# Attention's first loads, buffers and the experts' table: another order and other engines

## Chip, cores and metric

One core of a Trainium2 chip runs the whole kernel. Five engines work side by side, each on its own list of instructions: TensorE (PE), VectorE (DVE), ScalarE (ACT), GpSimd (POOL) and SyncE (SP, which here only issues DMAs). They wait for each other through semaphores. The metric is the device time of one execution in microseconds (us).

## What is computed

A batch of 8 samples. Each has 49 image patches, projected and normalised, and 512 words, embedded and passed through four encoder layers; together 561 tokens of 192 values. On these comes an attention layer and a layer of eight experts:

```
h = concatenate([tok(x), txt(x_txt)], axis=1)          # 8 x 561 x 192
h = h + attn(layernorm(h))                             # 12 heads of 64, own token masked out
h = h + ffn(layernorm(h))                              # 8 experts, the best 2 of each token

# attn(x)
qkv = x @ W_qkv.T ; q, k, v = split(qkv, 3)            # 12 heads each
dots = einsum('bhid,bhjd->bhij', q, k) * scale[head]
dots = where(diagonal, -987654321.0, dots)
out = einsum('bhij,bhjd->bhid', softmax(dots), v)
return out @ W_out.T + b_out
```

## The kernel before

The program has three phases, each a block of its own in which every engine has its instruction list; a phase begins on all engines when the one before has ended on all of them: `encoder_phase` (0 to about 2281 us), `attention_phase` (to about 3690 us) and `experts_phase`. They hand data over in DRAM: `tokens` (encoder to attention), `fused` (attention to experts) and `table` (one row of weights per expert and partition, 1024 rows of 11.5 KB, read by the experts by index).

**The encoder's end.** Encoder work runs in turns of two samples (`s` 0 and 1) over a written order of steps; `R_FINAL` is the last turn and `R_CLOSE` what is left behind it. In `encoder_phase` the list of SyncE is the function `steps` of the `sync` block: at step ("exp", 1, 0, 1) it stores a finished sample (L839), then loads two rows of norm parameters (L810, `load_rows(..., norm2_in)`). In `R_FINAL` the next things on SyncE's list are the two last stores of `h_out` (calls of `store` behind `steps(R_FINAL, 0)`, L839 again). GpSimd waits for `stored` of the other `s` before it writes `h_out` anew (L756). At its end SyncE waits for the last stores (L947 and on).

**Attention.** One sample at a time (`B` = 8), each over 5 tiles of tokens (four of 128 rows, one of 49) and 12 heads. The regions are `R_AHEAD` (what must run before the first sample's loop body), `R_FIRST`, `R_SECOND`, a loop of five, `R_FINAL` and `R_CLOSE`. `R_AHEAD` holds, in order: ("ln", 0) moments and ("ln", 1) normalising of the tokens on VectorE (L1376 to L1385, with the reciprocal root on GpSimd, L49 and L51), ("t", 0/1) transposes on TensorE (L1231) that ScalarE copies to `xT` (L1333), ("qk", ...) products for the first four heads (L1240), from which ScalarE and VectorE write q and k as a high part and a rest (L1338, L1340, L1410, L1413), SyncE's copies between partitions (`place`, L1123 to L1127), then the maxima and sums of four heads (L1268, L1271, L1430, L1320), `lse` and `maxt`. The v products, which need `wv`, the output product, which needs `wo`, and the addition of `b_out` on GpSimd (L1189) come only in `R_FIRST` or behind it.

**The start of attention, engine by engine.**
- SyncE: loads `ident`, `wqk`, `wv`, `wo`, `b_out`, `scales` (L1165), each counted on `fixed_in`; then the tokens of sample 0 (`load(0, loaded)`, L1116 and L1117); waits for `ready` 3.
- VectorE: sets `q_hm` and `k_l1` to 0 (L1439), the last columns of `q_hl` and `k_hh` (L1441), `vals` and `probs` of the last tile (L1443), three small ones (L1445), then rows 64 and 65 of `k_l1` to 1 (L1447); waits for `fixed_in` 96 (all six loads) and makes `eye16` and `mask16` from `ident` (L1452, L1453). Each of the two large memsets, the ones in `k_l1`, `eye16` and `mask16` count one on `ready`.
- GpSimd: sets `half` (L1204), waits for `fixed_in` 96 and `ready` 5.
- TensorE: waits for the same two.
- ScalarE: first issues seven DMAs that build `table` from the inputs `wup_rows`, `wdown_rows`, `bdown` and `bup_rows`, DRAM to DRAM (L1362, counted on `made`), then waits for the same two.

SyncE waits for `made` at the end of attention. In `q_hm`, partitions 0 to 63 take a copy of q's high part, partitions 64 and 65 the shifts of the softmax, and the rest stay 0; in `k_l1`, partitions 0 to 63 take k's rest and 64 and 65 hold 1, against the shifts. A product of the two sums over all 128 partitions.

## Time and profile before

| | us |
|---|---|
| runs | 4368.18, 4368.94, 4373.55 |
| median | 4368.94 |
| the profiled execution, its own time | 4374.97 |
| its span, first to last instruction | 4373.2 |
| busy in the span: PE, DVE, ACT, POOL | 3810.5, 2232.9, 2119.3, 1101.8 |
| mean granted clock of TensorE, of full | 0.924 |

How to read the rows below. All times are us from the span's start unless ns is written. A row of the timeline is: start, length, engine, line of the kernel, operation, output <- input, shape, count; in brackets, how long the engine was idle before it and what ended that ("issue": nothing that the profile shows). "ACTq", "SPq" are the queues of DMA instructions of those engines: their length is the time for issuing, not for the transfer; neighbouring rows of one kind are merged, from the first's start to the last's end. L1441 and the like are lines of the listing. "PEclk" is the granted clock of TensorE as a share of 2.4 GHz. "DMA share" is the mean busy share of the core's sixteen DMA engines. A row of DMA issues ends with the us from issue to landing.

### The profile page before, as it was taken

The page shows a single profiled execution, that of the slowest core. Times are in us where ns is not written, and L with a number is a line of the kernel's source. Part 1 is how long each engine was busy: PE and PEld are TensorE (multiplying, and loading weights), DVE is VectorE, ACT ScalarE, POOL GpSimd, SP SyncE. Part 2 cuts the span into 40 slices and gives each one's busy share as a digit, 9 for nine tenths or more (in the row PEclk, how much of TensorE's full clock was granted, in tenths as well). Part 3 has the DMA queues.
Part 4 walks back from the last instruction along what each step waited for, and adds up shares of the span by engine and source line. Part 5 has one row for each costly group of instructions (what it writes and reads, how often), then busy time and mean ns, then how long its engine had stood idle before and what let it go on. Part 6 is the DMA issues. An engine that isn't in the chain of part 4 may idle for free. (4 is left out here: it accounts for less than half of the span.)

```text
span 4373.2 us, 64449 instructions
## 1 busy us (share of the span) xinstructions
PE 3810.5 (87%) x21850; PEld 2532.1 (58%) x21850; DVE 2232.9 (51%) x3419; ACT 2119.3 (48%) x3230; POOL 1101.8 (25%) x1004
## 2 busy tenths in 40 slices
PE   4899999999999999999856999999999996408998
PEld 2455555555555555555534677666766774307887
DVE  6566666666666666666524444444444442213443
ACT  0554554554555545545414766755756663003332
POOL 5132332322332322323210000000000001063444
PEclk7899999999999999999977999999999998558999
DMA  7333233242343342333114111111111112335664
GB/s 174 93 101 105 87 106 102 87 117 87 90 119 93 94 117 79 101 108 92 48 48 116 31 34 27 31 35 23 35 31 24 37 28 96 103 112 161 148 145 107
DMA packets 265492, 368.62 MB, mean 84 GB/s; under 512 B 49616, under 2 KB 166400, under 8 KB 261824
## 3 DMA queue, kind: packets, MB, share of 16 engines
q1 hardware_dynamic: 232752, 285.52, 23.1%
q0 software_dynamic: 22960, 57.40, 5.8%
q10 hardware_dynamic: 9600, 23.26, 1.6%
q8 instruction: 118, 1.93, 0.2%
q14 instruction: 62, 0.51, 0.0%
HBM read 235.77 MB, written 116.32 MB: 81 GB/s over the span
## 5 line engine op out<-in xcount | busy, mean ns | idle before, releaser
L641 DVE TENSOR_REDUCE mx<-ring 128x2 f32<-128x1024 f32 x768 | 920.0, 1223 | 505.8 <-PE ring L404 502.8
L533 ACT ACTIVATE probs<-ring 128x1024 f32<-128x1024 f32 x768 | 767.2, 1024 | 418.0 <-PE ring L417 417.0
L1430 DVE TENSOR_REDUCE a_nmx<-a_ring 128x1 f32<-128x561 f32 (+1 forms) x480 | 341.6, 737 | 309.1 <-PE a_ring L1271 158.9
L1320 ACT ACTIVATE a_ring<-a_ring,a_nmx 128x561 f32<-128x561 f32 (+1 forms) x480 | 333.8, 695 | 197.8 <-DVE a_nmx L1430 194.8
L404 PE MATMUL ring<-k_stack,q_stack 48*128 48x512 f32 x1536 | 360.0, 481 | 63.5 <-ACT probs L533 23.1
L417 PE MATMUL ring<-q_stack,k_stack 64*128 64x512 f32 x1536 | 363.5, 490 | 51.9 <-DVE mx L641 39.2
L431 PE MATMUL acc<-probs,vals 128*32 128x512 f32 x3072 | 400.6, 642 | 1.3 <-ACT probs L533 1.3
L1201 POOL TENSOR_SCALAR_AFFINE_SELECT a_probs<-a_probs 128x256 f32<-128x256 f32 (+1 forms) x240 | 91.9, 383 | 1227.4 <-ACT a_probs L1352 1227.4
L1352 ACT ACTIVATE a_probs<-a_ring 128x561 f32<-128x561 f32 (+1 forms) x480 | 287.4, 637 | 169.2 <-PE a_ring L1268 166.4
L1268 PE MATMUL a_ring<-a_k_hh,a_q_hl 128*128 128x256 f32 (+1 forms) x960 | 311.1, 339 | 22.6 <-DVE a_q_hl L1410 11.0
L417 PEld LDWEIGHTS ring<-q_stack,k_stack 64*128 64x128 f32 x1536 | 142.6, 189 | 285.9 <-DVE mx L641 102.0
L404 PEld LDWEIGHTS ring<-k_stack,q_stack 48*128 48x128 f32 x1536 | 145.5, 191 | 279.7 <-issue 84.7
L1268 PE MATMUL a_ring<-a_q_hl,a_k_hh 128*128 128x256 f32 (+1 forms) x960 | 288.7, 326 | 10.4 <-ACT a_ring L1320 7.6
L477 PE MATMUL ring<-w,relu 128*128 128x192 f32 x1536 | 279.7, 332 | 1.4 <-ACT relu L540 1.4
L1288 PE MATMUL a_acc<-a_probs,a_vals 128*64 128x305 f32 (+1 forms) x1920 | 275.1, 413 | 0.1
L1268 PE MATMUL a_ring<-a_k_l,a_q_hm 128*128 128x256 f32 (+1 forms) x960 | 272.1, 292 | 0.0
L477 PEld LDWEIGHTS ring<-w,relu 128*128 128x128 f32 x1536 | 246.3, 190 | 33.6 <-issue 31.1
L1268 PE MATMUL a_ring<-a_q_hm,a_k_l 128*128 128x256 f32 (+1 forms) x960 | 264.4, 292 | 0.0
L1240 PE MATMUL a_ring<-a_xT,a_wqk 96*128 96x256 f32 (+1 forms) x768 | 217.9, 432 | 23.0 <-issue 11.5
L49 POOL TENSOR_SCALAR var_eps<-mv 128x4 f32<-128x4 f32 (+1 forms) x65 | 14.9, 229 | 844.8 <-DVE mv L576 844.5
L1888 ACT ACTIVATE m_hid<-m_ring,m_table 128x512 f32<-128x512 f32 x150 | 103.0, 686 | 254.3 <-PE m_ring L1867 254.3
L1837 POOL DMA_INDIRECT fused<-m_y,m_ids x100 | 167.9, 1679 | 213.8 <-DVE m_y L1920 198.6
(220 smaller groups left out, 6801.8 us busy)
## 6 DMA issues: line engine op xcount, KB each, us to landing
q_stack<-qk_scratch SPq DMA_DIRECT2D x576, 64.0 KB, 2.3
k_stack<-qk_scratch SPq DMA_DIRECT2D x576, 64.0 KB, 2.4
qk_scratch<-qk_hi SPq DMA_DIRECT2D x32, 768.0 KB, 3.6
qk_scratch<-qk_lo SPq DMA_DIRECT2D x32, 768.0 KB, 5.1
a_q_hm<-a_q_hl SPq DMA_DIRECT2D x48, 280.5 KB
a_k_hh<-a_k_hh SPq DMA_DIRECT2D x48, 280.5 KB
tokens<-h_out SPq DMA_DIRECT2D x33, 384.0 KB, 2.5
h_in<-tokens SPq DMA_DIRECT2D x32, 384.0 KB, 4.3
```

Source lines behind the costliest of these rows:

```text
L404: last = nc.tensor.matmul(buf[:, r, :], q_st[s][terms, t, P * i:P * i + P], k_st[s][terms, t, :], start=True, stop=True)
L417: last = nc.tensor.matmul(buf[:, r, :], k_st[s][terms, t, P * kt:P * kt + P], q_st[s][terms, t, :], start=True, stop=True)
L431: last = nc.tensor.matmul(acc[g % 2][32 * hh:32 * hh + 32, :], vals[s][:, kt, 4 * (n // 2) + hh, :], probs[n % 2][:, hh, j, :], start=(n % ...
L477: last = nc.tensor.matmul(buf[:, i // 2, D * (i % 2):D * (i % 2) + D], relu[:, k2, P * i:P * i + P], w2[:, k2, :], start=(k2 == 0), stop=( ...
L533: nc.scalar.activation(probs[n % 2][:, pair:pair + 2, x // 2, :], buf[:, :, :], ACT.Exp, scale=DK ** -0.5).then_inc(act, 1)
L641: nc.vector.tensor_reduce(mx[s][:, i, :].rearrange("p (r t) -> p r t", r=2)[:, :, t], buf[:, :, :], AX, ALU.max).then_inc(dve, 1)
L1240: last = nc.tensor.matmul(flat(buf)[:, n0:n0 + n], wqk[:, c, P * j:P * j + P], xT[:, c, n0:n0 + n], start=(c == 0), stop=(c == 1))
L1268: last = nc.tensor.matmul(flat(buf)[0:r, n0:n0 + w], a, b[:, n0:n0 + w], start=(m == 0), stop=(m == 1 and not masked))
L1288: last = nc.tensor.matmul(flat(acc)[DH * r:DH * r + DH, n0:n0 + w], vals[:, i, 2 * p + r, :], probs[i][:, r, n0:n0 + w], start=(i == 0), s ...
L1320: nc.scalar.activation(buf, buf, ACT.Exp, bias=nmx[0:r, i, h:h + 1], accum_out=sums[0:r, i, h:h + 1]).then_inc(act, 1)
L1352: nc.scalar.activation(probs[i][0:r, h % 2, :], flat(buf)[0:r, 0:N], ACT.Exp).then_inc(act, 1)
L1430: nc.vector.tensor_reduce(nmx[0:r, i, h:h + 1], flat(buf)[0:r, 0:N], AX, ALU.max, negate=True).then_inc(dve, 1)
```

## The change

- SyncE's loads in attention: the tokens of sample 0 first, then `ident`, `wqk` and `scales`, counted on `fixed_in`; then `wv`, `wo`, `b_out`, counted on a new semaphore `later_in`. It waits for `ready` 4 instead of 3.
- TensorE waits for `fixed_in` 48 and `ready` 4, runs `R_AHEAD`, and then waits for `later_in` 48. GpSimd waits for neither at the start, runs `R_AHEAD`, and then waits for `later_in` 48. ScalarE and VectorE wait for `fixed_in` 48 and `ready` 4 only.
- `q_hm` is set to 0 by GpSimd. VectorE sets all of `k_l1` to 1 at once, as the last of its memsets; the second memset on it is gone. `ready` now counts `q_hm`, `k_l1`, `eye16`, `mask16`.
- SyncE's copy of zeros into `q_hm`, partitions 64 and 65, is read from `q_hm`, partitions 66 and 67, instead of from `k_l1`.
- The seven DMAs of `table` go from ScalarE at attention's start to SyncE in the encoder's last turn, behind the load of the norm parameters at ("exp", 1, 0, 1). SyncE waits for `made` at the end of the encoder.

```
@@ encoder, sync block @@
+            def build_table():
+                rows = table[:, :].rearrange("(e p) c -> p e c", p=P)
+                up = dram["wup_rows"].rearrange("(e k) (c f) -> c k e f", e=EXPERTS, c=2)
+                for dst, src in ((rows[0:KC, :, 0:FF], up[0]), (rows[KC:P, :, 0:FF], up[1, 0:P - KC]),
+                                 (rows[0:D - P, :, FF:2 * FF], up[1, P - KC:KC]), (rows[D - P:P, :, FF:2 * FF], up[1, P - KC:KC]),
+                                 (rows[:, :, WDOWN:BDOWN], dram["wdown_rows"].rearrange("(e p) c -> p e c", p=P)),
+                                 (rows[:, :, BDOWN:BUP], dram["bdown"].partition_broadcast(P)),
+                                 (rows[:, :, BUP:ROW], dram["bup_rows"].rearrange("(e p) c -> p e c", p=P))):
+                    sp.dma_start(dst, src).then_inc(made, 16)
...
                             load_rows(turn // 4, 4, 6, norm2_in)
+                        if s == 1 and R is R_FINAL:
+                            build_table()
...
             store(R_CLOSE, 0, 1, 7, len(CLOSE))
+            sp.wait_ge(made, 16 * 7)
@@ attention, sync block @@
-                    sp.dma_start(q_hm[DH:DH + 2, heads, :].bitcast(F32), k_l1[DH + 2:DH + 4, heads, :].bitcast(F32)).then_inc(placed[p], 16)
+                    sp.dma_start(q_hm[DH:DH + 2, heads, :].bitcast(F32), q_hm[DH + 2:DH + 4, heads, :].bitcast(F32)).then_inc(placed[p], 16)
...
-            for dst, src in ((ident[:, :], dram["ident"]), (wqk[:, :, :], dram["a_wqk"]), (wv[:, :, :], dram["a_wv"]),
-                             (wo[:, :, :], dram["a_wo"]), (b_out[:, :, :], dram["a_bout"].partition_broadcast(P)),
-                             (scales[:, :], dram["a_scale"].partition_broadcast(P))):
-                sp.dma_start(dst, src).then_inc(fixed_in, 16)
             load(0, loaded)
-            sp.wait_ge(ready, 3)
+            for dst, src, done in ((ident[:, :], dram["ident"], fixed_in), (wqk[:, :, :], dram["a_wqk"], fixed_in),
+                                   (scales[:, :], dram["a_scale"].partition_broadcast(P), fixed_in),
+                                   (wv[:, :, :], dram["a_wv"], later_in), (wo[:, :, :], dram["a_wo"], later_in),
+                                   (b_out[:, :, :], dram["a_bout"].partition_broadcast(P), later_in)):
+                sp.dma_start(dst, src).then_inc(done, 16)
+            sp.wait_ge(ready, 4)
...
-            sp.wait_ge(made, 16 * 7)
@@ attention, gpsimd block @@
-            g.wait_ge(fixed_in, 96)
-            g.wait_ge(ready, 5)
-            for R in (R_AHEAD, R_FIRST, R_SECOND):
+            nc.gpsimd.memset(q_hm[:, :, :].bitcast(F32), 0.0).then_inc(ready, 1)
+            steps(R_AHEAD, 0)
+            g.wait_ge(later_in, 48)
+            for R in (R_FIRST, R_SECOND):
                 steps(R, 0)
@@ attention, tensor block @@
-            pe.wait_ge(fixed_in, 96)
-            pe.wait_ge(ready, 5)
-            for R in (R_AHEAD, R_FIRST, R_SECOND):
+            pe.wait_ge(fixed_in, 48)
+            pe.wait_ge(ready, 4)
+            steps(R_AHEAD, 0)
+            pe.wait_ge(later_in, 48)
+            for R in (R_FIRST, R_SECOND):
                 steps(R, 0)
@@ attention, scalar block: the seven DMAs of the table go @@
-                sc.dma_start(dst, src).then_inc(made, 16)
-            sc.wait_ge(fixed_in, 96)
-            sc.wait_ge(ready, 5)
+            sc.wait_ge(fixed_in, 48)
+            sc.wait_ge(ready, 4)
@@ attention, vector block @@
-            for t in (q_hm, k_l1):
-                nc.vector.memset(t[:, :, :].bitcast(F32), 0.0).then_inc(ready, 1)
+            for s in (mm, dve, ln, stored):
+                v.sem_inc(s, BASE)
             for t in (q_hl, k_hh):
                 nc.vector.memset(t[:, :, N:NE].bitcast(F32), 0.0)
             for t in (vals[:, 4, :, :], probs[4][:, :, :]):
                 nc.vector.memset(t, 0.0)
             for t in (nmx, sums, mv):
                 nc.vector.memset(t[:, :, :], 1.0)
-            v.wait_ge(ready, 2)
-            nc.vector.memset(k_l1[DH:DH + 2, :, :].bitcast(F32), 1.0).then_inc(ready, 1)
-            for s in (mm, dve, ln, stored):
-                v.sem_inc(s, BASE)
-            v.wait_ge(fixed_in, 96)
-            v.wait_ge(ready, 3)
+            nc.vector.memset(k_l1[:, :, :].bitcast(F32), 1.0).then_inc(ready, 1)
+            v.wait_ge(fixed_in, 48)
             nc.vector.tensor_copy(eye16[:, :], ident[:, :]).then_inc(ready, 1)
             nc.vector.tensor_scalar(mask16[:, :], ident[:, :], -BIG, None, ALU.mult).then_inc(ready, 1)
-            v.wait_ge(ready, 5)
+            v.wait_ge(ready, 4)
```

## Rows read from the trace of the kernel before

**Rows 1.** Waits of 2276 to 2372 us: who <- releaser: total, times, longest.
```profile
ACT a_xT L1333 <- issue: 65.8, 1, 65.8
...
DVE a_stats L1376 <- DMA a_tok<-tokens: 3.3, 1, 3.3
```

**Rows 2.** Timeline, ScalarE and its queue: start, length, instruction, idle before.
```profile
2281.44 11.03 ACTq L1362 DMA_DIRECT2D expert_table<-in_wup_rows  x4
...
2310.25 15.69 ACTq L1362 DMA_DIRECT2D expert_table<-in_bup_rows  x1
...
2326.07 1.16 ACT L1333 ACTIVATE a_xT<-a_ring 96x561 f32<-96x561 f32 x2 [65.78 <-issue]
```

**Rows 3.** Timeline, the chain from tokens to the first product.
```profile
2308.59 1.39 DVE L1376 BATCH_NORM_STATS2 a_stats<-a_tok 128x6 f32<-128x192 f32 x5 [3.25 <-DMA a_tok<-tokens]
...
2314.10 2.57 PE L1231 MATMUL a_ring<-a_ident,a_tok 128*96 128x128 f32 x10 [45.62 <-DVE a_tok L1385]
...
2327.28 10.87 PE L1240 MATMUL a_ring<-a_xT,a_wqk 96*128 96x256 f32 x32 [10.62 <-ACT a_xT L1333]
```

**Rows 4.** Timeline, SyncE's queue: three of the eight loads.
```profile
2281.38 0.34 SPq L1165 DMA_DIRECT2D a_ident<-in_ident  x1
...
2281.77 0.42 SPq L1165 DMA_DIRECT2D a_wqk<-in_a_wqk  x1
...
2284.97 0.47 SPq L1116 DMA_DIRECT2D a_tok<-tokens  x1
```

**Rows 5.** Timeline, VectorE's buffers.
```profile
2282.86 5.68 DVE L1439 MEMSET a_q_hm<- 128x6744 f32 x1 [8.85 <-issue]
...
2295.53 0.07 DVE L1441 MEMSET a_q_hl<- 128x12 f32 x1
...
2297.68 0.07 DVE L1445 MEMSET a_mv<- 128x10 f32 x1
...
2299.19 5.68 DVE L1447 MEMSET a_k_l<- 2x6744 f32 x1 [1.44 <-issue]
...
2305.12 0.22 DVE L1453 TENSOR_SCALAR mask<-a_ident 128x128 bf16<-128x128 f32 x1
```

**Rows 6.** Windows: stretch, length, busy PE to POOL, PEclk, DMA share, GB/s.
```profile
2171.00:2226.00 55.00, 43.84 (x258) 25.73 (x256) 10.37 (x32) 25.20 (x30) 11.86 (x10) 0.90 0.04 11
...
2285.00:2308.00 23.00, 0.00 (x0) 0.00 (x0) 17.15 (x12) 0.00 (x0) 0.00 (x0) 0.50 1.01 336
...
2331.00:2333.00 2.00, 2.00 (x6) 1.47 (x6) 0.80 (x2) 1.45 (x2) 0.00 (x0) 0.50 0.15 34
2333.00:2335.00 2.00, 2.00 (x9) 1.54 (x8) 0.80 (x1) 0.58 (x1) 0.00 (x0) 0.88 0.42 88
```

**Rows 7.** DMA of 2281 to 2335: queue's share; issues, KB, us to landing.
```profile
q10 hardware_dynamic: 5232, 11.82, 74.2%
...
a_wqk<-in_a_wqk SPq DMA_DIRECT2D x1, 1152.0 KB, 8.6
...
a_scales<-in_a_scale SPq DMA_DIRECT2D x1, 6.0 KB, 15.7
```

**Rows 8.** DMA of the whole run, two large loads of a later stage.
```profile
p_xn<-normed SPq DMA_DIRECT2D x2, 3456.0 KB, 20.1
...
r_h<-fused SPq DMA_DIRECT2D x3, 1152.0 KB, 6.4
```

**Rows 9.** Groups on GpSimd by form: xcount | busy, mean ns.
```profile
L756 POOL TENSOR_TENSOR h<-yn,enc_rows 128x768 f32<-128x768 f32 x32 | 58.7, 1835 | 44.1 <-DVE yn L604 44.1
...
L714 POOL CAST w_hi<-w 128x1536 fp32r<-128x1536 f32 x16 | 23.5, 1466 | 327.8 <-PE ring L360 283.1 <-issue 44.7
```

**Rows 10.** Timeline, the encoder's end: SyncE's queue and GpSimd.
```profile
2170.70 0.44 SPq L810 DMA_DIRECT2D enc_rows<-in_enc_rows  x1
...
2226.66 51.67 SPq L839 DMA_DIRECT2D tokens<-h_out  x2
...
2274.17 1.80 POOL L756 TENSOR_TENSOR h_out<-yn,enc_rows 128x768 f32<-128x768 f32 x1 [1.45 <-DVE yn L604]
```

More of the change, by code:

```diff
@@ L243, with encoder_phase @@
     closes = staticmethod(last_part)
-def encoder_phase(nc, dram, tokens):
+def encoder_phase(nc, dram, tokens, table):
     TURNS = LAYERS * B // 2
@@ L313, in encoder_phase @@
         stacked = [[sem(f"stacked{s}_{g}") for g in range(3)] for s in range(2)]
-        ones_set, tick = sem("ones_set"), sem("tick")
+        ones_set, tick, made = sem("ones_set"), sem("tick"), sem("made")
         h_dram = tokens[0:B * N, :].rearrange("(b n) d -> b n d", n=N)[:, IMG:N, :].rearrange(
@@ L1042, in rows_of, with attention_phase @@
     return (v[:, 0:4 * P, :].rearrange("b (i p) d -> b p i d", p=P)[b], v[:, 4 * P:N, :][b])
-def attention_phase(nc, dram, tokens, fused, table):
+def attention_phase(nc, dram, tokens, fused):
     start = {n: BASE for n in Attention.names}
@@ L1088, in attention_phase @@
         acc = ctx.enter_context(nc.psum_tensor("a_acc", [P, 2, 512], F32))
-        fixed_in, ready, loaded, loaded_again, mm, act, dve, ln, pool, stored = (sem(n) for n in (
-            "fixed_in", "ready", "loaded", "loaded_again", "mm", "act", "dve", "ln", "pool", "stored"))
+        fixed_in, later_in, ready, loaded, loaded_again, mm, act, dve, ln, pool, stored = (sem(n) for n in (
+            "fixed_in", "later_in", "ready", "loaded", "loaded_again", "mm", "act", "dve", "ln", "pool", "stored"))
         placed = [sem(f"placed{p}") for p in range(PAIRS)]
         max_in = [sem(f"max_in{g}") for g in range(GROUPS)]
-        rst, pool_res, tick, made = sem("rst"), sem("pool_res"), sem("tick"), sem("made")
+        rst, pool_res, tick = sem("rst"), sem("pool_res"), sem("tick")
         sems = {"mm": mm, "act": act, "dve": dve, "pool": pool}
@@ L1354, in _ @@
             sc.sem_inc(act, BASE)
-            rows = table[:, :].rearrange("(e p) c -> p e c", p=P)
-            up = dram["wup_rows"].rearrange("(e k) (c f) -> c k e f", e=EXPERTS, c=2)
-            for dst, src in ((rows[0:KC, :, 0:FF], up[0]), (rows[KC:P, :, 0:FF], up[1, 0:P - KC]),
-                             (rows[0:D - P, :, FF:2 * FF], up[1, P - KC:KC]), (rows[D - P:P, :, FF:2 * FF], up[1, P - KC:KC]),
-                             (rows[:, :, WDOWN:BDOWN], dram["wdown_rows"].rearrange("(e p) c -> p e c", p=P)),
-                             (rows[:, :, BDOWN:BUP], dram["bdown"].partition_broadcast(P)),
-                             (rows[:, :, BUP:ROW], dram["bup_rows"].rearrange("(e p) c -> p e c", p=P))):
-                sc.dma_start(dst, src).then_inc(made, 16)
-            sc.wait_ge(fixed_in, 96)
-            sc.wait_ge(ready, 5)
+            sc.wait_ge(fixed_in, 48)
+            sc.wait_ge(ready, 4)
             for R in (R_AHEAD, R_FIRST, R_SECOND):
@@ L1938, in build @@
     table = nc.dram_tensor("expert_table", [EXPERTS * P, ROW], F32, kind="Internal").ap()
-    encoder_phase(nc, dram, tokens)
-    attention_phase(nc, dram, tokens, fused, table)
+    encoder_phase(nc, dram, tokens, table)
+    attention_phase(nc, dram, tokens, fused)
     experts_phase(nc, dram, fused, table, out.rearrange("b n d -> (b n) d"))
```

## The prediction

> **What bounds the kernel now.** The change touches one seam, the start of attention, and one quiet stretch before it, so I read views in that order. The waits of 2276 to 2372 us come first [rows 1]: ScalarE stands still 65.8 us before its first work in attention, and the releaser is given as "issue", so nothing that another engine did ended it. Second, the timeline of ScalarE's own queue in that stretch [rows 2]: seven DMA instructions that build the experts' table, from 2281.44 to 2310.25 + 15.69 = 2325.94, and the first activation at 2326.07. The engine was held by its own issuing. TensorE had its transposes ready at 2314.10 + 2.57 = 2316.67 and goes on only at 2327.28 [rows 3]. Third, the queue of SyncE and the buffers on VectorE [rows 4, 5], to see what is late next: tokens are issued last, at 2284.97, and VectorE waits for them until 2308.59 [rows 3]. The row of waits gives this only 3.3 us [rows 1], because VectorE was writing buffers before; it is a second chain right behind the first. Fourth, the DMA engines [rows 6, 7]: they are full (share 1.01) from 2285 to 2308 and the table's queue took 74.2% of 54 us, 40 us of all sixteen, for 11.82 MB. TensorE has 2.57 us of work in all the time until 2327: the table's whole transfer is laid beside nothing.
>
> **The change part by part.** All sums are made on the profiled execution: span 4373.2 us, its own time 4374.97 us, median of the runs 4368.94 us (6.0 us less). I take the difference off the median, since a difference of two points in one trace has no offset in it.
>
> (a) The table leaves ScalarE. It removes seven instructions and 44.5 us of issuing [rows 2] from the front of that engine. What is late next is the other chain: tokens landed, moments, normalised rows, transposes. From the first BATCH_NORM_STATS2 at 2308.59 to the last transpose at 2316.67 it takes 8.08 us; the second of ScalarE's two copies (1.16 us for both) has to follow the last transpose, 0.58 us, and the product starts 0.05 us after a copy [rows 2, 3]. So 8.7 us from the start of the moments, called T, to the first product. With T left at 2308.59 the product would start at 2317.3 and (a) alone would be worth 10 us; the rest is how early T becomes.
>
> (b) T now waits for four things: tokens, the three first loads, VectorE's own buffers, GpSimd's buffer.
> Tokens go first, at about 2281.4. Even behind nothing but their own 421 KB they are no limit: a load of 1152 KB lands after 6.4 us [rows 8], so tokens are there before 2288.
> First loads (identity, wqk, scales): 384 + 36.8 + 64 + 1152 = 1637 KB on one queue. The two large loads of the trace ran at 1152 / 6.4 = 180 and 3456 / 20.1 = 172 KB per us with no table beside them [rows 8]; 1637 KB takes 9.1 to 9.5 us and wqk lands at about 2290.9. Today it lands 8.6 us after its issue at 2281.77, 2290.4, beside the table [rows 4, 7]. The scales follow it with 6 KB. No row shows how late so small a broadcast is alone; from below it costs nothing, from above it takes again the 15.7 us from issue [rows 7] that it took behind wv, wo and b_out: the issues of the tokens, the identity and wqk last 0.3 to 1 us each [rows 4], so 2283.7 + 15.7 = 2299.4. I take under 1.7 us, the slack to VectorE's end below, as wv and wo are now behind it.
> VectorE: the q_hm memset (5.68 us) goes to GpSimd, the second writing of k_l1 on two partitions (5.68 us again, since the price goes by the elements of a partition) is gone, because all of k_l1 is written once with 1 [rows 5]. What stays: the small memsets, 2295.53 to 2297.75 = 2.22 us; k_l1, 5.68 us; the two copies of the identity, 0.47 us from the end of the memset at 2304.87 to 2305.34; and one gap of 1.4 us without a releaser, as stands before the last memset [rows 5]. 2282.86 + 2.22 + 1.4 + 5.68 + 0.47 = 2292.6. Without the gap 2291.2.
> GpSimd: 6744 elements per partition. No row has a large memset there. Its cheapest large instruction, a cast of 1536 elements, takes 1.466 us, 0.95 ns each: 6.4 us, end at 2288. Its dearest, two inputs of 768 elements, takes 1.835 us, 2.39 ns each: 16.1 us, end at 2297.6 [rows 9]. A memset reads nothing, so the cast is the nearer row: hidden behind VectorE, at no cost; with the dear price it costs 5.0 us. If both engines' writes shut each other out, VectorE's 5.68 us starts when GpSimd ends and T is 2288 + 5.68 + 0.5 + 2.2 = 2296.4.
> No row has the two engines' memsets side by side. The Trainium skill says (SBUF — State Buffer, section "Who interferes with whom") that a VectorE instruction with at most one SBUF input and outside the two-port modes doesn't contend with GpSimd, which would leave T where the memsets' own lengths put it; a locked pair would give the later T just worked out, 3.8 us more.
> So T = 2292.7 and the first product at 2301.4 instead of 2327.28: 25.9 us.
>
> (c) Waits that are added: TensorE and GpSimd wait for wv, wo and b_out (1248 KB) behind the first maxima. They land at about 2290.9 + 1248 / 175 = 2298, and the first user is more than 30 us after the first product; behind TensorE's wait stands the whole first batch, behind GpSimd's the masks of its probabilities. Both are passed at once. If that cover were gone, each us of lateness would count in full. SyncE's small copy into q_hm reads other zeros; the same 8.8 KB.
>
> (d) TensorE's clock. In the products' beginning the granted clock is 0.50 (1.2 GHz) and gets to 0.88 in 2333 to 2335 [rows 6]: 5.7 us at half speed, after 10.6 us in which TensorE did nothing behind its transposes [rows 3]. Now that idle time is 0.6 us. Bounds: nothing, or all of it, 2.9 us. I take 1.0, since copies, subtractions and DMAs stand between the products.
>
> (e) The table goes to SyncE in the encoder's last turn, behind the issue of enc_rows at 2170.70 + 0.44. All seven instructions are issued there. SyncE's next is a store at 2226.66; what waits for that store is GpSimd's writing of h_out at 2274.17 (through the wait on `stored`), and behind it the second of the two stores in that row, whose issue ends at 2226.66 + 51.67 = 2278.33 [rows 10]. The queue of SyncE has the table ahead of these two stores. The stretch 2171 to 2226 has a DMA share of 0.04 [rows 6], so the table, 40 us of all engines, is done at about 2213: 13 us before anyone queues behind it and 60 us before anyone waits. Issuing takes no longer than the transfer, as it does now (44.5 us). Cost: 0. The encoder has in that window two transfers of the instruction queue; no engine is shown waiting for them. Bounds 0 and two gaps like the one of 1.4 us [rows 5], 2.8 us.
>
> Sum: 25.9 + 1.0 = 26.9, taken as 27: 4368.9 - 27 = **4342 us** (span 4346).
>
> **The rivals.**
> Buffers late: GpSimd at the dear price, or the two shut each other out. T = 2296.4 to 2297.7, gain 21 to 23.2: 4347. For: no row of either. Against: a memset has no input. 0.14.
> The loads don't come early (the change doesn't do what its order says): the scales land last again, T = 2299.9, gain 2327.3 - 8.7 - 2299.9 = 18.7: 4350. For: 15.7 us for 6 KB in the trace [rows 7]. Against: what was ahead of it there (wv, wo, b_out and the table) now is behind or gone. 0.10.
> More than forecast: the clock stays at its upper level from the first product and there is no gap in VectorE: T at 2291.3 and 2.9 us, in all 30.2 us: 4339. 0.10.
> Slower: the table chokes SyncE's queue. From 2171.1 it has 103 us until GpSimd needs the store's landing (2274) and about 107 us until the last store; beyond, each us counts in full, and the phases are 27 us ahead. It is slower than before from 134 us on, a rate under 11.82 MB / 134 us = 88 GB/s, and at 79 GB/s (150 us) it would give 4369 + 16 = 4385. For: long issues, up to 15.69 us for one instruction [rows 2]. Against: 336 GB/s were moved with the table among it [rows 6]. A drain of 120 to 134 us would end within 0.2%. 0.04 for slower, 0.04 for the same.
>
> **How the numbers follow.** Forecast 0.58, and the four rivals 0.14, 0.10, 0.10 and 0.08 (both outcomes of the last). Low end: 4339 less 2 us of scatter, as the runs shown differ by 5 us. High end: 4350 with the encoder's 2.8 us, 4353. That leaves out the last rival and some of the tails. 0.2% (8.7 us) is about what a measurement of this kernel can tell from no change. Faster by more: 0.92; within: 0.04; slower: 0.04.
>
> **What would show it.** In the trace of after: no DMA issues on ScalarE's queue at attention's start, and seven on SyncE's from about 2171, done well before 2226; DMA share near 1 there and no TensorE wait that is new in the encoder; first BATCH_NORM_STATS2 at about 11.3 us after attention's first instruction and the first product 8.7 us later; GpSimd's memset near 6.4 us. The forecast is wrong if the GpSimd row is near 16 us, if VectorE's copy of the identity waits for a DMA, if the first product is over 25 us behind attention's first instruction (forecast 20), or if the encoder's last store moves.

## The result and the profile after

The changed kernel takes 4344.07 us in the median of 5 runs (4336.45 to 4348.50), the kernel before 4368.18 us in 5 runs (4364.14 to 4373.55). The ratio is 0.9943, with a 95% interval from 0.9929 to 0.9958: 25 us less (18 to 31), where 27 were forecast and 4342 us. Run once more later, beside other kernels, it gave 0.9944 (0.9932 to 0.9957).

The profiled execution of after is the shortest of its five (4336.45 us, span 4334.6), and its span is 38.6 us under that of before. That is not all the change's. The row that answers to the load of enc_rows in [rows 10] starts at 2160.90 instead of 2170.70: 9.8 us of the difference lie in the encoder ahead of the first changed instruction, where the two programs are the same (the changed kernel, run once more, has that row at 2168.39). So the readings below count from attention's first instruction on GpSimd (2281.37 us before, 2270.36 after).

The timeline of attention's start after; it answers to [rows 3] and [rows 5]:

```profile
2270.63 5.72 POOL L1220 MEMSET a_q_hm<- 128x6744 f32 x1 [0.16 <-issue]
...
2274.42 5.68 DVE L1454 MEMSET a_k_l<- 128x6744 f32 x1 [1.35 <-issue]
2281.40 0.23 DVE L1456 CAST eye<-a_ident 128x128 bf16<-128x128 f32 x1 [1.30 <-DMA a_scales<-in_a_scale]
...
2281.79 1.39 DVE L1384 BATCH_NORM_STATS2 a_stats<-a_tok 128x6 f32<-128x192 f32 x5
...
2287.21 2.57 PE L1245 MATMUL a_ring<-a_ident,a_tok 128*96 128x128 f32 x10 [29.77 <-DVE a_tok L1393]
...
2290.50 10.02 PE L1254 MATMUL a_ring<-a_xT,a_wqk 96*128 96x256 f32 x32 [0.73 <-ACT a_xT L1349]
```

The moments (the first BATCH_NORM_STATS2) start at 11.4 us instead of 27.2, the first product at 20.1 instead of 45.9, and TensorE's idle time before it falls from 10.62 to 0.73 us. The waits of ScalarE and VectorE, answering to [rows 1]:

```profile
ACT a_xT L1349 <- PE a_ring L1245: 39.9, 2, 39.4
...
DVE eye L1456 <- DMA a_scales<-in_a_scale: 1.3, 1, 1.3
```

ScalarE still has nothing to do for 39.4 us, across the end of the encoder, but now it waits for TensorE's transposes and not for its own issuing. VectorE waits 1.3 us for the scales: the new limit of the start is a load of 6 KB.

The queue of SyncE in the encoder's last turn (timeline), and the load of the DMA engines there (windows: busy of PE, PEld, DVE, ACT and POOL, then granted clock, DMA share, GB/s). These answer to [rows 2], [rows 10] and the first of [rows 6]:

```profile
2160.90 0.44 SPq L810 DMA_DIRECT2D enc_rows<-in_enc_rows  x1
2161.39 5.56 SPq L849 DMA_DIRECT2D expert_table<-in_wup_rows  x4
2166.99 0.64 SPq L849 DMA_DIRECT2D expert_table<-in_wdown_rows  x1
2167.68 15.68 SPq L849 DMA_DIRECT2D expert_table<-in_bdown  x1
2183.40 16.03 SPq L849 DMA_DIRECT2D expert_table<-in_bup_rows  x1
2215.74 0.40 SPq L839 DMA_DIRECT2D tokens<-h_out  x1
```

```profile
2161.00:2199.00 38.00, 32.83 (x188) 17.53 (x188) 5.10 (x15) 24.03 (x28) 7.76 (x6) 0.94 1.02 289
2199.00:2216.00 17.00, 10.49 (x69) 8.11 (x67) 5.26 (x17) 1.33 (x3) 4.87 (x4) 0.81 0.39 86
```

Issuing takes 38.0 us, the DMA engines are full meanwhile and TensorE is busy 32.83 of 38 us beside them, as much as in the same stretch of before (32.82 of the 38 us from 2171.00). Landings (KB, us from issue), against [rows 7]:

```profile
a_wqk<-in_a_wqk SPq DMA_DIRECT2D x1, 1152.0 KB, 8.3
...
expert_table<-in_bup_rows SPq DMA_DIRECT2D x1, 24.0 KB, 24.9
...
a_scales<-in_a_scale SPq DMA_DIRECT2D x1, 6.0 KB, 9.3
```

The last part of the table lands at 2183.40 + 24.9 = 2208.3, 7 us before SyncE's next store.

### The profile page after: what moved, and what is told of

It reads as the page before. It is cut to its first block and busy times, and to the rows that moved or that the text cites. A ratio compares the mean times of both kernels' runs of the same rounds, so it can differ in the third digit from the quotient of the medians.

```text
span 4334.6 us, 64446 instructions
## 1 busy us (share of the span) xinstructions
PE 3795.0 (88%) x21850; PEld 2523.9 (58%) x21850; DVE 2221.4 (51%) x3417; ACT 2118.7 (49%) x3230; POOL 1107.4 (26%) x1005
## 5 line engine op out<-in xcount | busy, mean ns | idle before, releaser
L533 ACT ACTIVATE probs<-ring 128x1024 f32<-128x1024 f32 x768 | 767.1, 1024 | 411.3 <-PE ring L417 410.5
L404 PE MATMUL ring<-k_stack,q_stack 48*128 48x512 f32 x1536 | 358.3, 479 | 63.8 <-ACT probs L533 23.2
L49 POOL TENSOR_SCALAR var_eps<-mv 128x4 f32<-128x4 f32 (+1 forms) x65 | 14.8, 228 | 843.1 <-DVE mv L576 842.8
L1254 PE MATMUL a_ring<-a_xT,a_wqk 96*128 96x256 f32 (+1 forms) x768 | 218.2, 433 | 12.8 <-issue 11.3
```

Of the source, the lines that this page charges most:

```text
L404: last = nc.tensor.matmul(buf[:, r, :], q_st[s][terms, t, P * i:P * i + P], k_st[s][terms, t, :], start=True, stop=True)
L533: nc.scalar.activation(probs[n % 2][:, pair:pair + 2, x // 2, :], buf[:, :, :], ACT.Exp, scale=DK ** -0.5).then_inc(act, 1)
L1254: last = nc.tensor.matmul(flat(buf)[:, n0:n0 + n], wqk[:, c, P * j:P * j + P], xT[:, c, n0:n0 + n], start=(c == 0), stop=(c == 1))
```

## The experiments

The start of attention repeats to half a us in the two traces of the changed kernel, the whole execution only to some ten: the kernel before gave 4350.84 to 4376.65 us in 30 runs on one chip. So each kernel is read twice, by three points of its trace in us from attention's first instruction (the first maxima are VectorE's first TENSOR_REDUCE), and by its time against the kernel before on the same chip.

| kernel | moments | first product | first maxima | ratio to before (95% interval) |
|---|---|---|---|---|
| before | 27.2 | 45.9 | 59.8 | 1 |
| changed | 11.4 | 20.1 | 32.8 | 0.9943 (0.9929 to 0.9958) |
| changed, once more | 11.8 | 20.5 | 33.1 | 0.9944 (0.9932 to 0.9957) |
| the table's move alone | 24.0 | 32.8 | 46.7 | 0.9983 (0.9967 to 0.9999) |
| all but the table's move | 14.6 | 43.4 | 57.8 | 1.0002 (0.9989 to 1.0016) |
| changed, buffers as before | 24.3 | 33.0 | 45.7 | 0.9974 (0.9961 to 0.9987) |
| changed, loads as before | 13.2 | 21.9 | 34.9 | 0.9955 (0.9944 to 0.9966) |
| table issued behind attention's loads | 11.2 | 19.9 | 57.5 | 1.0005 (0.9994 to 1.0016) |
| before, table's small parts first | 24.0 | 32.8 | 50.8 | one run: 4351.16 us |
| changed, table three times | 10.6 | 19.3 | 33.1 | 1.0013 (1.0003 to 1.0023) |
| changed, scales ahead of wqk | 14.8 | 23.5 | 36.3 | one run: 4347.91 us |
| moments first, scales ahead of wqk | 3.6 | 14.5 | 28.3 | 0.9943 (0.9927 to 0.9959) |
| moments first, wqk ahead | 3.5 | 12.5 | 26.2 | 0.9917 (0.9901 to 0.9932) |

The theory: two chains end the start of attention, ScalarE's issuing of the table and, 10 us behind, what the moments wait for. The rivals: the table is everything; the parts simply add; only the issuing engine matters.

**The table's move alone.** To the kernel before:

```diff
+                        if s == 1 and R is R_FINAL:      # encoder, SyncE
+                            build_table()
...
-                sc.dma_start(dst, src).then_inc(made, 16)    # attention, ScalarE
```

> The kernel before with one part of the change alone: the seven DMAs of the experts' table are issued by SyncE in the encoder's last turn. Loads, buffers and waits of attention stay as before. All times count from attention's first instruction (before: first product at 45.9 us, moments at 27.2; after the whole change: 20.1 and 11.4). Theory (two chains end almost together, and the second is VectorE's buffers and the tokens): ScalarE is free, and the moments start when VectorE's buffers are set, at 24.0 us (2305.34 - 2281.37), since with no table beside them 2.9 MB of loads land by about 17 us; the first product stands at 24.0 + 8.7 = 32.7 us, a gain of 13 us, time about 13 us under before. Rival (the table is everything): first product at 20 us, gain 25 us, as the whole change. Rival (tokens behind all loads are the limit): moments later than 24.5 us with VectorE waiting for a DMA.

Moments at 24.0 us and first product at 32.8, as the theory had them. The gain at the product is 13.1 us, not 25.8: half of the change. VectorE's buffers are the next limit. The time fell by 0.4 to 14.4 us: the interval holds the theory's 13 and not the rival's 25, and its middle, 7 us, is under both. The trace is the sharper witness here.

**All but the table's move.** To the changed kernel:

```diff
-                            build_table()
...
+                sc.dma_start(dst, src).then_inc(made, 16)    # attention, ScalarE, as before
```

> The changed kernel with one part undone: the seven DMAs of the experts' table are issued by ScalarE at attention's start, as before. Tokens come first, later loads are awaited later, buffers are set on two engines. Theory (ScalarE is held by its own issuing, whatever the rest does): the transposes are done at about 16 to 18 us from attention's first instruction and ScalarE's first copy starts only at 44 to 45 us; first product at 45 to 46 us, time within 2 us of before. Rival (the parts add): first product 10 us or more earlier than before.

The timeline of ScalarE and its queue:

```profile
2308.01 15.92 ACTq L1366 DMA_DIRECT2D expert_table<-in_bup_rows  x1
...
2324.06 1.16 ACT L1337 ACTIVATE a_xT<-a_ring 96x561 f32<-96x561 f32 x2 [63.29 <-issue]
```

The last issue ends at 2323.93 and the first activation follows at once, though the transposes began at 20.0 us. The first product is at 43.4 us, 2.5 us earlier than before (45 to 46 had been expected; the issuing itself ends 2.5 us sooner), and the time is the same. Alone this half gives 2.5 us, the other 13.1, both 25.8: the parts don't add, each uncovers the other.

**Buffers as before, and loads as before.** Both are the changed kernel with one part undone:

```diff
-            nc.gpsimd.memset(q_hm[:, :, :].bitcast(F32), 0.0).then_inc(ready, 1)
...
+            for t in (q_hm, k_l1):
+                nc.vector.memset(t[:, :, :].bitcast(F32), 0.0).then_inc(ready, 1)
...
-            nc.vector.memset(k_l1[:, :, :].bitcast(F32), 1.0).then_inc(ready, 1)
+            nc.vector.memset(k_l1[DH:DH + 2, :, :].bitcast(F32), 1.0).then_inc(ready, 1)
```

```diff
-            load(0, loaded)
-            for dst, src, done in ((ident[:, :], dram["ident"], fixed_in), (wqk[:, :, :], dram["a_wqk"], fixed_in),
...
+            for dst, src in ((ident[:, :], dram["ident"]), (wqk[:, :, :], dram["a_wqk"]), (wv[:, :, :], dram["a_wv"]),
+                             (wo[:, :, :], dram["a_wo"]), (b_out[:, :, :], dram["a_bout"].partition_broadcast(P)),
+                             (scales[:, :], dram["a_scale"].partition_broadcast(P))):
+                sp.dma_start(dst, src).then_inc(fixed_in, 16)
+            load(0, loaded)
...
-            pe.wait_ge(fixed_in, 48)
+            pe.wait_ge(fixed_in, 96)
```

> The changed kernel with the buffers as before: VectorE sets q_hm and k_l1 to 0 and two partitions of k_l1 to 1, GpSimd sets none. Loads and table as changed. Theory (VectorE's buffers are the bound once the table is gone): moments at 24.0 us from attention's first instruction instead of 11.4, first product at 32.7 instead of 20.1, and the time 12.6 us over the changed kernel, 12 us under before. Rival (loads are the bound, the buffers lie beside them): first product within 2 us of the changed kernel's.

> The changed kernel with the loads in the order of before (identity, wqk, wv, wo, b_out, scales, tokens last) and everything awaited at the start. Buffers and table as changed. In the changed kernel the first loads landed 11.0 us after attention's first instruction and b_out 14.7 us. Theory: tokens, 421 KB at about 175 KB per us behind all of that, land at about 17 us; the moments start at 17.2 us instead of 11.4, the first product at 26 us, 6 us over the changed kernel. Rival (the order matters little without the table's traffic): within 2 us of the changed kernel.

The buffers behave as expected: the first product falls back by 12.9 us to 33.0 and the time with it (0.9974 against 0.9943). This run takes back both savings on VectorE, the buffer moved to GpSimd and the second writing of k_l1; which gives how much was not split. The loads don't behave as expected: their order, with the waits that go with it, is worth 1.8 us, not 6, which is inside the 2 us of the rival that it matters little, and the time doesn't tell it from the changed kernel (0.9955 against 0.9943). Their timeline says why:

```profile
2282.98 0.41 SPq L1130 DMA_DIRECT2D a_tok<-tokens  x1
...
2291.52 0.23 DVE L1454 CAST eye<-a_ident 128x128 bf16<-128x128 f32 x1 [2.40 <-DMA a_scales<-in_a_scale]
...
2292.60 1.39 DVE L1382 BATCH_NORM_STATS2 a_stats<-a_tok 128x6 f32<-128x192 f32 x5 [0.72 <-DMA a_tok<-tokens]
```

All 2891 KB, the tokens last, are there by 2292.6 - 2279.4 = 13.2 us: 219 KB per us over the whole, where 172 to 180 were taken from [rows 8]. What the changed kernel waits for at its start, the scales last, is there at 11.0 us, only 2.2 us sooner.

**The table behind attention's loads.** Changed kernel, but SyncE issues the table in attention:

```diff
-                            build_table()
...
                 sp.dma_start(dst, src).then_inc(done, 16)       # attention's loads
+                sp.dma_start(dst, src).then_inc(made, 16)       # the table's seven
             sp.wait_ge(ready, 4)
```

> The changed kernel, but the table's seven DMAs are issued by SyncE at attention's start behind all loads, instead of in the encoder. It asks whether the gain needs a quiet stretch for the table, or only that ScalarE doesn't issue it. Theory (SyncE's later copies between partitions stand behind the table, in SyncE's list and in its queue): the first product is early, at 20 to 21 us from attention's first instruction, but the first maxima, which wait for those copies, stand at about 55 us instead of 31.9, and the time is 20 to 25 us over the changed kernel, about that of before. Rival (only the issuing engine matters): first maxima at 32 to 34 us and the time that of the changed kernel.

The timeline of SyncE's queue, then a row of TensorE's:

```profile
2308.27 14.40 SPq L1175 DMA_DIRECT2D expert_table<-in_bup_rows  x1
2322.78 4.82 SPq L1123 DMA_DIRECT2D a_q_hm<-a_q_hl  x1
```

```profile
2333.47 0.55 PE L1278 MATMUL a_ring<-a_k_hh,a_q_hl 128*128 128x256 f32 x1 [25.95 <-DMA a_k_hh<-a_k_hh]
```

The first product is as early as in the changed kernel. But SyncE gets to the first copy between partitions only when the table is issued, and TensorE then idles 25.95 us for that copy. The whole gain is gone (1.0005). "Only the issuing engine matters" has fallen: SyncE too holds up what stands behind the table on its list. The place in the encoder pays because nothing is due on that queue for longer than the table takes. Whether a queue with nothing due would do as well inside attention was not run.

**What the long issues are.** The kernel before, table on ScalarE, other order:

```diff
-            for dst, src in ((rows[0:KC, :, 0:FF], up[0]), (rows[KC:P, :, 0:FF], up[1, 0:P - KC]),
+            for dst, src in ((rows[:, :, BUP:ROW], dram["bup_rows"].rearrange("(e p) c -> p e c", p=P)),
+                             (rows[:, :, BDOWN:BUP], dram["bdown"].partition_broadcast(P)),
+                             (rows[0:KC, :, 0:FF], up[0]), (rows[KC:P, :, 0:FF], up[1, 0:P - KC]),
...
-                             (rows[:, :, WDOWN:BDOWN], dram["wdown_rows"].rearrange("(e p) c -> p e c", p=P)),
-                             (rows[:, :, BDOWN:BUP], dram["bdown"].partition_broadcast(P)),
-                             (rows[:, :, BUP:ROW], dram["bup_rows"].rearrange("(e p) c -> p e c", p=P))):
+                             (rows[:, :, WDOWN:BDOWN], dram["wdown_rows"].rearrange("(e p) c -> p e c", p=P))):
```

> The kernel before with the table's seven DMAs still on ScalarE at attention's start, but in another order: the two small ones (bup_rows 24 KB, bdown 768 KB, 1024 rows each) first, the large wdown_rows last. It asks what the 12.2 and 15.7 us of issuing were. Theory (an issue is held until the queue has room, so it is long for what stands last, whatever it is): the small ones issue in 1 us each, a later one is long, and ScalarE is free earlier, at 25 to 35 us instead of 44.5, as the rows still queued then are long ones; the first product follows the moments (27 us) and stands at 36 to 40 us. Rival (small rows are slow to issue by themselves): bup_rows and bdown take 12 to 16 us each at the front too, and ScalarE is held for 44 us as before.

Timeline of ScalarE's queue:

```profile
2281.72 0.71 ACTq L1362 DMA_DIRECT2D expert_table<-in_bup_rows  x1
...
2282.46 0.69 ACTq L1362 DMA_DIRECT2D expert_table<-in_bdown  x1
...
2283.18 16.27 ACTq L1362 DMA_DIRECT2D expert_table<-in_wup_rows  x4
...
2299.48 5.03 ACTq L1362 DMA_DIRECT2D expert_table<-in_wdown_rows  x1
```

That timeline shows what the issues were: the same bup_rows that took 15.69 us [rows 2] takes 0.71 at the front. An issue is long because of what is queued ahead of it; how full the queue is, no row shows. ScalarE is free at 22.9 us instead of 44.6, sooner than the 25 to 35 expected. The first product comes at 32.8 us, not at 36 to 40, since with ScalarE's issuing out of the way VectorE's buffers end the wait, as in the table's move alone: moments at 24.0 in both. So the order of seven lines is worth the same 13.1 us there as the move. Of this 9.0 us are left at the first maxima (50.8 against 59.8): TensorE waits 5.86 us for a copy between partitions instead of 1.78, with the DMA engines still full of the table (share 1.03 in 2330 to 2332). All this is read from one trace; its one time can't carry it.

**The table three times.** The changed kernel with two more tables, that nobody reads, built behind the first:

```diff
-                            build_table()
+                            for one_table in (table, table_b, table_c):
+                                build_table(one_table)
```

> The changed kernel with the table built three times in the encoder's last turn, into three tensors of which the last two are read by nobody: it takes away the cover of the move. One table took 47 us from its issue to its last landing. Theory (the table costs nothing until it is still in the queue when the last stores are issued): three take 120 to 135 us; the encoder's last stores stand behind them, and the phase ends about 12 to 25 us late, so the time is 12 to 25 us over the changed kernel, while the encoder's compute before the last store keeps its pace. Rival (the traffic slows the encoder's compute itself): TensorE's stretch from the table's issue to its last product grows by some us already. Rival (cover is longer): no change.

Windows of the encoder and its timeline on GpSimd:

```profile
2168.00:2205.00 37.00, 31.82 (x181) 16.23 (x180) 5.10 (x15) 23.33 (x28) 7.31 (x6) 0.93 1.02 298
2205.00:2268.00 63.00, 37.45 (x179) 31.00 (x177) 12.84 (x41) 7.47 (x10) 11.54 (x9) 0.73 1.02 272
```

```profile
2298.03 1.80 POOL L756 TENSOR_TENSOR h_out<-yn,enc_rows 128x768 f32<-128x768 f32 x1 [28.60 <-DMA tokens<-h_out]
```

With full DMA engines for 100 us the encoder's compute keeps its pace: from the load of enc_rows to GpSimd's last reciprocal root (L51) it is 100.95 us with three tables, and 99.74 to 101.0 us in the four traces without one there (before, all but the move, small parts first, behind the loads). Then the store stands behind the tables and GpSimd waits 28.60 us for it, a little over the expected 12 to 25: from 2167.9 to the last landing at 2297.1, three tables take 129 us, 43 each. The time rises by 0.7 points, 30 us, against the changed kernel. The cover of the move is real and ends where the store on the same queue is needed, 101.5 us behind the table's first issue.

**A further step.** On the changed kernel, moments before the large buffer, and each wait at its first user:

```diff
+            moments(R_AHEAD, 0)                       # VectorE
+            normalise(R_AHEAD, 0)
             nc.vector.memset(k_l1[:, :, :].bitcast(F32), 1.0).then_inc(ready, 1)
...
-            pe.wait_ge(fixed_in, 48)                  # TensorE, start
-            pe.wait_ge(ready, 4)
+            pe.wait_ge(ident_in, 16)
...
+                            if R is R_AHEAD:
+                                pe.wait_ge(fixed_in, 32)
...
+                        if R is R_AHEAD and step == ("max", 0, 0):
+                            pe.wait_ge(ready, 4)
...
-            for dst, src, done in ((ident[:, :], dram["ident"], fixed_in), (wqk[:, :, :], dram["a_wqk"], fixed_in),
-                                   (scales[:, :], dram["a_scale"].partition_broadcast(P), fixed_in),
+            for dst, src, done in ((ident[:, :], dram["ident"], ident_in), (scales[:, :], dram["a_scale"].partition_broadcast(P), fixed_in),
+                                   (wqk[:, :, :], dram["a_wqk"], fixed_in),
```

> A further step on the changed kernel. VectorE takes the moments and normalises as soon as tokens have landed and its small buffers are set, and only then sets k_l1; TensorE's transposes wait for the identity alone, its first product for wqk and scales, its first maxima for the large buffers; the scales are loaded ahead of wqk. Theory (the moments need tokens only): moments at about 4.2 us from attention's first instruction, first product at 4.2 + 8.7 = 12.9 us instead of 20.1, if wqk has landed (9.6 us in the changed kernel); k_l1 is set by about 15.5 us, before VectorE's first rest of a product. Time 7 us under the changed kernel, 32 us under before. Rival (tokens or wqk land later than that, as all first loads share sixteen engines): first product at 15 us or later and under 5 us gained. Rival (VectorE's memset then delays the first rests): product early, first maxima not.

The moments are at 3.6 us, even earlier than expected, and the first product at 14.5 instead of 12.9. The row of waits names the load that ScalarE waits for:

```profile
ACT a_xT L1352 <- DMA a_wqk<-in_a_wqk: 34.4, 1, 34.4
```

wqk landed 11.5 us after its issue, at 13.3, where it had been 9.6. The scales had been put ahead of it, on the belief that 6 KB are nothing. Two kernels tell whether they are the cause. The first is this one with wqk ahead of the scales:

```diff
-            for dst, src, done in ((ident[:, :], dram["ident"], ident_in), (scales[:, :], dram["a_scale"].partition_broadcast(P), fixed_in),
-                                   (wqk[:, :, :], dram["a_wqk"], fixed_in),
+            for dst, src, done in ((ident[:, :], dram["ident"], ident_in), (wqk[:, :, :], dram["a_wqk"], fixed_in),
+                                   (scales[:, :], dram["a_scale"].partition_broadcast(P), scales_in),
...
+                        if R is R_AHEAD and step == ("qk", "q", 0):
+                            sc.wait_ge(scales_in, 16)
...
-            sc.wait_ge(fixed_in, 32)
```

> As the kernel with moments first, but wqk is loaded ahead of the scales, the scales count on a semaphore of their own that only ScalarE's and VectorE's first work on a product awaits, and ScalarE's copies of the transposes await no load. With moments first and the scales ahead, the moments stood at 3.6 us from attention's first instruction and the transposes at 9.2, but wqk landed at 13.3 us (9.6 in the changed kernel) and the first product stood at 14.5. Theory (the small broadcast holds up what is queued behind it): wqk lands at 9.6 to 10 us, the first product stands at 12.5 us, 7.6 us before the changed kernel's, and the time is 5 to 8 us under the changed kernel. Rival (wqk is late because something else took the DMA engines): first product still at 14 us or later.

The second is the changed kernel with the scales ahead of wqk:

```diff
-            for dst, src, done in ((ident[:, :], dram["ident"], fixed_in), (wqk[:, :, :], dram["a_wqk"], fixed_in),
-                                   (scales[:, :], dram["a_scale"].partition_broadcast(P), fixed_in),
+            for dst, src, done in ((ident[:, :], dram["ident"], fixed_in),
+                                   (scales[:, :], dram["a_scale"].partition_broadcast(P), fixed_in), (wqk[:, :, :], dram["a_wqk"], fixed_in),
```

> The changed kernel with the scales (6 KB, broadcast to 128 partitions) loaded ahead of wqk instead of behind it; nothing else differs. Theory (the small broadcast holds the queue up): wqk lands at about 13 us from attention's first instruction, and the moments start at 13.3 us instead of 11.4. Rival (6 KB cost nothing where they stand): the moments start at 10.1 us, when VectorE has set k_l1, 1.3 us earlier than in the changed kernel.

The landing of wqk there (DMA), and VectorE's timeline:

```profile
a_wqk<-in_a_wqk SPq DMA_DIRECT2D x1, 1152.0 KB, 12.6
```

```profile
2293.53 0.23 DVE L1456 CAST eye<-a_ident 128x128 bf16<-128x128 f32 x1 [4.63 <-DMA a_wqk<-in_a_wqk]
```

With only that one load moved ahead, VectorE waits 4.63 us for wqk and the moments start at 14.8, 3.3 us later (13.3 us had been expected); wqk lands 12.6 us from its issue instead of 8.3, at 14.4 instead of 9.6 us. Behind wqk the same 6 KB land at 11.0. Why 6 KB cost that much was not found. With wqk ahead and the moments first, wqk lands at 10.0, the first product stands at 12.5 us, as expected, and the median is 4331.37 us against 4339.09 of the changed kernel on the same chip, 7.7 us less. This version is the best of all; its interval and that of the changed kernel just touch (0.9932). With the scales ahead the step didn't show in the time at all.

> The changed kernel itself once more, beside the others: moments at 10.6 to 11.4 us from attention's first instruction, first product at 19.3 to 20.1 us, time 0.3 to 0.7% under before. If the encoder's length differs between its executions by 10 us, the spread of its times is that, and not the change's.

## Why the prediction was right

By its own steps:

- (a) ScalarE held by its own issuing: shown by all but the table's move, which keeps 15.92 us of issuing right before the first activation. "Alone worth 10 us with T left" was said under its condition; alone it is worth 13.1 at the product, since without the table T also comes forward, from 27.2 to VectorE's 24.0 us.
- (b) T at 11.3 us and the first product at 20.0: measured 11.4 and 20.1, and 10.6 to 11.8 and 19.3 to 20.5 in the other three traces with this start; the 8.7 us summed between the two measured 8.7. But that T came right to 0.1 us is luck: two errors met. VectorE's buffers ended at 9.7 us, not 10.8, and the scales came 1.3 us behind them, at 11.0, which the text named as a sign of being wrong. The limit was the DMA by a little, not the memset.
- The 1.1 us on VectorE look like a gap that the sum counts once too often. What the prediction took for idle time before a memset seems to be part of the memset, by these rows of timelines (the first two of before, the third of after, the fourth of the changed kernel with buffers as before):

```profile
2289.89 5.68 DVE L1439 MEMSET a_k_l<- 128x6744 f32 x1 [1.35 <-issue]
2296.60 0.99 DVE L1443 MEMSET a_probs<- 128x1122 f32 x1 [0.18 <-issue]
```

```profile
2270.82 0.07 DVE L1449 MEMSET a_q_hl<- 128x12 f32 x1 [7.86 <-PEq L259]
```

```profile
2273.26 5.68 DVE L1448 MEMSET a_q_hm<- 128x6744 f32 x1 [9.25 <-issue]
```

  The gap grows with the elements, 0.18 us at 1122 and 1.35 at 6744, and from the start of q_hm's row [rows 5] to that of k_l1's it is 7.03 us. The last two rows are the first memsets at the same point of VectorE's list: the small one starts 0.5 us behind attention's first instruction, the large one 1.9. So the row of a memset on VectorE seems to start late, and 6744 elements to cost 7.03 us, of which the row shows 5.68; this is a reading of rows, and no run tests it. The prediction's start at 2282.86 already held the gap of q_hm's memset, and it then added that of k_l1's.
- GpSimd's memset: 5.72 us, under the 6.4 of the nearer row; the dear price and the 4347 us with it fall. VectorE's large memset, gap and row, is 1.35 and 5.68 us beside it, as alone (above and [rows 5]); the two rows lie side by side for 1.9 us. So here the Trainium skill's rule (SBUF — State Buffer, "Who interferes with whom") agrees with the trace. That rival's gain of 21 to 23.2 us holds the clock's 1.0 us at its upper end and not at its lower, and the next rival's 18.7 leaves it out; neither changes which came true.
- Loads: wqk at 9.6 us was forecast 9.5, so the rate of 172 to 180 KB per us held for the first 1637 KB (171). Over all loads in the old order it was 219, and so that order, which the expectation gave 6 us, is worth 1.8. The rival in which the scales land last is close to that run: it costs 2 us and not 7.
- (c) The added waits: passed at once; the loads they wait for land at 14.7 us (b_out, issued at 3.2, 11.5 us to landing), the first maxima need nothing of them and stand at 32.8.
- (d) The clock: 1.0 us was credited to a shorter idle time before the products. After shows 12.7 us from the first product to the first maxima instead of 13.9, and the window of 2294.5 to 2296.5 (4 to 6 us behind the product) has 0.88 of the clock. The changed kernel run once more needs 12.6 us. But the kernel with three tables has the same start and the same idle time, and needs 13.8 us, and so does the table's move alone (13.9, idle 0.72):

```profile
2294.50:2296.50 2.00, 2.00 (x9) 1.63 (x8) 1.08 (x2) 1.45 (x2) 0.00 (x0) 0.88 0.00 0
2302.50:2304.50 2.00, 1.90 (x15) 1.58 (x14) 1.51 (x3) 0.51 (x1) 0.00 (x0) 1.00 0.57 123
```

```profile
2329.00:2331.00 2.00, 2.00 (x8) 1.52 (x7) 1.48 (x2) 1.20 (x2) 0.00 (x0) 0.70 0.00 0
2337.00:2339.00 2.00, 2.00 (x9) 1.81 (x10) 0.96 (x2) 0.00 (x0) 0.00 (x0) 0.50 0.55 118
```

The first fence is the changed kernel, the second that with three tables (first product at 2324.60), in windows 4 and 12 us behind the first product. In the second the clock rises later and is back at 0.50 (1.2 GHz) at the first maxima, as in before. The two have the same instructions there, so the term is not shown to be the change's, and where it came true it may be luck; what decides between the two courses was not found.
- (e) Free cover in the encoder: shown twice. Once by the lengths above (with the table in it the same stretch takes 98.6 to 101.0 us), once by tripling. What was mis-sized is the drain (47 us to the last landing instead of 42), and in the slower rival the break-even: in the tripled table 129 us hold GpSimd up by 28.6 us, 3.6 more than the 25 gained, and the time is 1.0013 (1 to 10 us over before). So it lies near 125 us by the trace, 119 to 128 by the time, not at 134: the delay counts from the 101.5 us at which GpSimd needs the store.

The sum held: the terms that carried it, 45.9 to 20.1 us, repeat in every trace with this start, and the times agree with the gains at the first maxima within their intervals but for the loads as before (24.9 us there, 15 to 24 by the time). What stays open is what makes an execution 10 us longer or shorter than the next of the same kernel. It is not the encoder alone: from the first maxima to the end the changed kernel takes 2031 us in one trace and 2020 in the other. No run here looked for it.

## What to carry to other kernels

When an engine stands idle with "issue" as releaser at the start of a phase, look at its own DMA queue: issuing can hold the engine while the transfers ahead drain (here 44.5 us of issuing), so a bulk transfer belongs on a queue whose engine has nothing due, in a stretch with idle DMA engines, and no store or copy that is needed soon may stand behind it. Before costing one half of such an edit, ask what is late next: here one half gave 13.1 us at the product, the other 2.5, both together 25.8. And let each wait stand at its first user, with the work that is due first ahead of the buffers that are needed later; the two together brought the first product another 7.6 us forward.

## What was not expected of the hardware

- A DMA's issue time says little of that DMA: 24 KB in 1024 rows took 15.69 us to issue behind the rest of the table and 0.71 us ahead of it.
- A load of 6 KB, one row broadcast to 128 partitions, delays what stands behind it in the queue: 1152 KB landed at 14.4 us instead of 9.6, and at 13.3 instead of 10.0 with the moments first.
- A memset's row on VectorE seems to start late: 5.68 us for 6744 elements per partition, but 7.03 us from one start to the next. GpSimd's row for as many elements is 5.72 us, and what lies ahead of it only 0.16; it was not run alone, and nothing waited for it to check its length.
- DRAM to DRAM copies of the table at a DMA share of 1.02 leave the encoder's compute as it is, for 100 us on end (100.95 us with them, 99.74 to 101.0 without).
